# Softplus as one function of ScalarE in a selective-scan and int8 feed-forward layer

## What is computed

```python
u = layernorm(x)
xp = u @ x_proj_w.T                    # 96 columns: 64 for the step, 16 for B, 16 for C
delta = softplus(xp[:, :64] @ dt_proj_w.T + dt_proj_b)      # [row, 512]
dA  = exp(delta[..., None] * -exp(A_log))                   # [row, 512, 16]
dBu = delta[..., None] * Bm[:, None, :] * u[..., None]
h = dA_t * h + dBu_t                   # over the rows of a sequence, 512 x 16 states
y = sum_n h * C_t  +  u * D
x = x + y
x = x + int8_matmul(quantize(layernorm(x)), weight_q) * scales + bias
```

## Time and profile before

| | us |
|---|---|
| three runs | 3096.60, 3097.05, 3104.22 |
| median | 3097.05 |
| the profiled execution, its own time | 3105.25 |
| its span, first to last instruction | 3103.4 |
| steady stretch, 30 chunks (100.59 to 2942.38) | 2841.79, or 94.73 a chunk |
| busy in that stretch, a chunk: VectorE, ScalarE, TensorE, GpSimd | 92.85, 92.15, 87.00, 86.23 |

### The profile page before, as it was taken

How to read it: one execution, slowest core, us unless ns; L and a number is a source line. 1 busy time by engine, 2 the same in 40 slices (tenths; PEclk the granted TensorE clock), 3 DMA queues, 4 the chain that set the end, 5 groups by cost and what they waited for, 6 DMA issues and landing times.

```text
span 3103.4 us, 57860 instructions
## 1 busy us (share of the span) xinstructions
PE 2800.9 (90%) x21569; PEld 2423.8 (78%) x21632; DVE 2978.6 (96%) x3234; ACT 2952.2 (95%) x4930; POOL 2766.5 (89%) x1488
## 2 busy tenths in 40 slices
PE   5899999999999999999999899998999998999986
PEld 4778878788877788777887777887778877878875
DVE  5999999999999999999999999999999999999996
ACT  7999999999999999999999999999999999999984
POOL 3899989899899988999889998999889998899987
PEclk8999999999999999999999999999999999999998
DMA  4221222221222212222212222122222122221111
GB/s 151 66 79 56 79 80 79 80 92 42 80 92 79 79 57 79 79 79 93 79 43 79 93 79 79 58 78 80 79 82 91 42 82 90 79 79 66 56 65 41
DMA packets 111225, 236.01 MB, mean 76 GB/s; under 512 B 56097, under 2 KB 56097, under 8 KB 94562
## 3 DMA queue, kind: packets, MB, share of 16 engines
q1 hardware_dynamic: 110946, 232.32, 21.4%
HBM read 195.92 MB, written 36.37 MB: 75 GB/s over the span
## 4 chain that ended last, share of the span: by engine, by line
PE 31%; DVE 30%; ACT 29%; issue 9%; POOL 1%; DVEq 0%; POOLq 0%; ACTq 0%
DVE A L635 23%; ACT A L400 12%; ACT DB L413 10%; PE PB L519 9%; PE Y L538 9%; PE PB L516 6%; PE PM L559 3%; DVE ST L650 2%; DVE X L640 2%; ACT Z L465 2%; ACT QT L491 1%; ACT Z L461 1%; PE PM L550 1%; ACT C L483 1%; DVE AM L676 1%
## 5 line engine op out<-in xcount | busy, mean ns | idle before, releaser
L359 POOL TENSOR_TENSOR A<-A,CB 128x2048 f32<-128x2048 f32 x512 | 2327.9, 4560 | 17.8 <-DVE A L635 5.6
L635 DVE TENSOR_TENSOR_SCAN A<-A,CAR,PB 128x512 f32<-128x512 f32 x1536 | 1871.9, 1262 | 36.0 <-PE PB L519 12.5
L400 ACT ACTIVATE A<-DEL,an 128x512 f32<-128x512 f32 x2048 | 1366.5, 711 | 4.6 <-PE Y L538 3.0
L519 PE MATMUL PB<-idf,DB 128*128 128x128 f32 x6656 | 1030.7, 280 | 183.7 <-DVE A L635 175.1
L538 PE MATMUL Y<-idf,A 128*128 128x128 f32 x8192 | 1129.0, 275 | 2.0 <-POOL A L359 2.0
L413 ACT ACTIVATE DB<-XN,BC 128x512 f32<-128x512 f32 x1664 | 1113.1, 710 | 4.8 <-PE PB L519 2.7
L519 PEld LDWEIGHTS PB<-idf,DB 128*128 128x128 f32 x6656 | 768.8, 143 | 425.4 <-DVE A L635 306.3
L538 PEld LDWEIGHTS Y<-idf,A 128*128 128x128 f32 x8192 | 954.8, 143 | 32.6 <-issue 16.4
L635 DVE TENSOR_TENSOR_SCAN A<-A,PB 128x512 f32<-128x512 f32 x512 | 596.9, 1204 | 34.2 <-PE PB L519 14.4
L516 PE MATMUL PB<-DG,XN 128*128 128x128 f32 x3072 | 421.9, 281 | 50.9 <-DVE A L635 48.0
L516 PEld LDWEIGHTS PB<-DG,XN 128*128 128x128 f32 x3072 | 372.2, 191 | 87.1 <-issue 51.2
(11 more groups left out here) (69 smaller groups left out, 1678.3 us busy)
## 6 DMA issues: line engine op xcount, KB each, us to landing
CB<-c_rows SPq DMA_DIRECT2D x128, 1024.0 KB, 4.8
X<-in_x SPq DMA_DIRECT2D x32, 1024.0 KB, 5.6
out<-X SPq DMA_DIRECT2D x32, 1024.0 KB, 4.3
DG<-b_diag SPq DMA_DIRECT2D x32, 768.0 KB, 6.9
b_diag<-DG SPq DMA_DIRECT2D x2, 768.0 KB, 9.3
b_diag<-BC SPq DMA_DIRECT2D x96, 2.0 KB, 5.1
C<-in_wq SPq DMA_DIRECT2D x1, 1024.0 KB, 11.5
DB<-in_wq SPq DMA_DIRECT2D x1, 1024.0 KB, 13.3
```

The lines of the kernel that those rows point to most:

```text
L359: gp.tensor_tensor(A[s % NA][:, :, :], A[s % NA][:, :, :], CB[:, s % (4 * NG), :].unsqueeze(1).broadcast_to([128, KB, L]), ALU.mult).then_ ...
L400: act.activation(A[s % NA][:, g, :], DEL[k % 2][:, g, :], ACT.Exp, scale=an[:, g, n:n + 1])\
L519: i = pe.transpose(PB[u % 2][:, j * 128:(j + 1) * 128], DB[(scaled(s) - 1) % ND][:, j, g * 128:(g + 1) * 128], idf[:, :])
L635: dve.tensor_tensor_scan(A[s % NA][:, g, :], A[s % NA][:, g, :], PB[(4 * s + g) % 2][:, :], init, ALU.mult, ALU.add).then_inc(s_scan, 1)
```

## The change

The three tasks of ScalarE and the one of VectorE become one task of ScalarE, which reads PSUM and writes DEL. The buffer Z and three semaphores go. The waits that the VectorE pass had (for DEL's readers of two chunks ago) go over to ScalarE, and `d_t` now waits for ScalarE's pass.

```diff
 PLACES = {
-        "delta": (-356, -304, -239, -144),
+        "delta": (-283, -268, -228, -192),
...
-        Z = sb("Z", [128, 2, L])
...
-            def z_out(p, g):
-                n = KB * p + g
-                act.wait_ge(s_dt, n + 1)
-                if n >= 2:
-                    act.wait_ge(s_del, n - 1)
-                act.activation(Z[:, g % 2, :], bank(p, g)[:, :], ACT.Abs).then_inc(s_z, 1)
-
-            def sp_exp(p, g):
-                act.wait_ge(s_z, KB * p + g + 1)
-                act.activation(Z[:, g % 2, :], Z[:, g % 2, :], ACT.Exp, scale=-1.0).then_inc(s_e, 1)
-
-            def sp_ln(p, g):
-                act.wait_ge(s_e, KB * p + g + 1)
-                act.activation(Z[:, g % 2, :], Z[:, g % 2, :], ACT.Ln, bias=1.0).then_inc(s_ln, 1)
+            def delta(p, g):
+                act.wait_ge(s_dt, KB * p + g + 1)
+                if g == 0 and p >= 2:
+                    act.wait_ge(s_exp, 4 * NS * (p - 1))
+                    act.wait_ge(s_dlt, T * (p - 1))
+                act.activation(DEL[p % 2][:, g, :], bank(p, g)[:, :], ACT.Softplus).then_inc(s_del, 1)
...
-            def delta(p, g):
-                n = KB * p + g
-                dve.wait_ge(s_ln, n + 1)
-                if g == 0 and p >= 2:
-                    dve.wait_ge(s_exp, 4 * NS * (p - 1))
-                    dve.wait_ge(s_dlt, T * (p - 1))
-                dve.scalar_tensor_tensor(DEL[p % 2][:, g, :], bank(p, g)[:, :], 0.0, Z[:, g % 2, :],
-                                         ALU.max, ALU.add).then_inc(s_del, 1)
```

More of the change, by code:

```diff
@@ L7 @@
 PLACES = {
[L8 to L22, removed]
-        "delta": (-356, -304, -239, -144),
-        "dl_t": (-143, -113, -98, -92),
@@ L25 @@
[L25 to L51, removed]
[8 rows of a table removed]
[L60 to L67, removed]
+        "act_b": (-98, -93, -90, -89, -82, -82, -72, -72, -61, -34, -19, 20, 25, 29, 33, 33, 39, 124, 194,
@@ new lines @@
+        196, 198, 202, 210, 227, 317, 320, 321, 329, 334, 400, 428, 431, 445, 446, 450, 462, 463, 485, 490,
+        648, 654, 662, 713, 713, 714, 722, 728, 733, 753, 818, 888, 892),
+        "addbias": (1640,),
+        "amax": (1433, 1460, 1474, 1482),
+        "ascale": (1457,),
+        "b_c": (-451,),
+        "bc_out": (-368,),
+        "carry": (-12, 81, 163, 206, 331, 345, 428, 498, 508, 551, 630, 671, 675, 813, 834, 971),
+        "centre": (1287, 1295, 1296, 1398),
+        "d_t": (-331, -260, -255, -188),
@@ new lines @@
+        "decay": (-133, -107, -100, -91, -82, -77, -74, -62, -25, -22, -16, -15, 41, 49, 99, 99, 102, 104,
+        150, 155, 176, 185, 193, 197, 235, 237, 277, 278, 305, 317, 335, 376, 419, 430, 430, 448, 451, 505,
+        509, 529, 568, 584, 592, 609, 609, 647, 651, 688, 689, 699, 699, 716, 783, 792, 795, 796, 798, 806,
+        814, 815, 817, 847, 855, 859),
+        "delta": (-283, -268, -228, -192),
+        "dl_t": (-172, -141, -97, -78),
+        "du": (-84, -47, -36, -28),
+        "final": (2053, 2155),
@@ new lines @@
+        "gather": (1088, 1131, 1165, 1181),
+        "load": (-2162,),
+        "load_c": (-700, -667, -636, -486),
+        "load_g": (-670,),
+        "magic": (1529, 1555, 1584, 1590),
+        "newton0": (-1172,),
+        "newton1": (1175,),
+        "q_mm": (1785, 1826, 1884, 1930),
+        "q_t": (1569, 1605, 1631, 1700),
+        "qt_out": (1630, 1666, 1705, 1752),
+        "root0": (-1174,),
+        "root1": (1246,),
+        "scale_out": (1861, 1887, 1963, 2026),
+        "scales": (1586,),
@@ new lines @@
+        "scan": (29, 39, 41, 47, 54, 56, 56, 56, 66, 66, 74, 94, 119, 145, 154, 234, 244, 247, 255, 266, 283,
+        290, 291, 301, 307, 355, 368, 416, 432, 451, 462, 464, 538, 569, 591, 597, 598, 610, 611, 611, 618,
+        626, 626, 632, 634, 640, 661, 669, 757, 810, 819, 839, 844, 859, 873, 875, 940, 954, 954, 967, 973,
+        974, 984, 1016),
+        "stats0": (-1293, -1273, -1270, -1187),
+        "stats1": (1150, 1201, 1201, 1236),
+        "store": (1380,),
+        "store_c": (-883,),
@@ L68 @@
+        "store_g": (-901,),
[8 rows of a table added]
+        "times_c": (62, 142, 175, 299, 331, 371, 456, 531, 592, 620, 664, 690, 758, 876, 889, 972),
+        "weights": (-185,),
+        "x_p": (-557, -538, -512, -503),
+        "x_t": (-816, -715, -654, -634),
+        "xn": (-940, -932, -921, -921),
+        "xp_out": (-422,),
+        "xt_out": (-779, -718, -676, -641),
 }
@@ L185, in build @@
         s_dt = sem("s_dt")
-        s_z = sem("s_z")
-        s_e = sem("s_e")
-        s_ln = sem("s_ln")
         s_del = sem("s_del")
@@ L492, in qt_out @@
                                bias=-MAGIC).then_inc(s_qe, 1)
-            run(root0=lambda p, i: root(p, 0), root1=lambda p, i: root(p, 1), xn=xn, xt_out=xt_out, z_out=z_out,
-                sp_exp=sp_exp, sp_ln=sp_ln, xp_out=lambda p, i: xp_out(p), bc_out=lambda p, i: bc_out(p),
+            run(root0=lambda p, i: root(p, 0), root1=lambda p, i: root(p, 1), xn=xn, xt_out=xt_out, delta=delta,
+                xp_out=lambda p, i: xp_out(p), bc_out=lambda p, i: bc_out(p),
                 centre=centre, magic=magic, qt_out=qt_out, decay=decay, act_b=act_b)
@@ L689, in scale_out @@
                                          ALU.mult, ALU.mult).then_inc(s_o, 1)
-            run(stats0=lambda p, i: stats(p, 0, i), stats1=lambda p, i: stats(p, 1, i), gather=gather, delta=delta,
-                du=du, amax=amax, scale_out=scale_out, scales=lambda p, i: scales(p), weights=lambda p, i: weights(p),
+            run(stats0=lambda p, i: stats(p, 0, i), stats1=lambda p, i: stats(p, 1, i), gather=gather, du=du, amax=amax, scale_out=scale_out, scales=lambda p, i: scales(p), weights=lambda p, i: weights(p),
                 scan=scan)
```

## The result

| | before | changed |
|---|---|---|
| median of 4 runs, us | 3097.02 | 3280.02 |
| lowest to highest | 3096.60 to 3104.22 | 3279.30 to 3286.04 |
| the profiled execution and its span | 3105.25, 3103.4 | 3279.93, 3278.1 |

The ratio is 1.0583, with a 95% interval of 1.0564 to 1.0602. The forecast was 3261 us, with a range of 3185 to 3390.

What follows compares the result with a forecast made beforehand. VectorE and ScalarE were both taken as nearly full, with ScalarE setting the pace afterwards. Chunks of 100.06 us added 159.9 us over 30, edges 4, giving 3269.2, less 8.2 to the median: 3261 us, range 3185 to 3390.

Steps and rivals of the forecast that it cites:

- The bound: Steady chunks: VectorE and ScalarE both nearly full before; after, ScalarE sets the pace, VectorE's 2.4 us saving being worth nothing.
- What ScalarE loses and gains: ScalarE, per chunk: 4.76 us saved on Exp and Ln passes, 11.04 us added by eight table loads of 1.38.
- My sum without waits: Steady chunk: old period 94.73 us, less 4.76 for passes, plus 11.04 for loads, less 2.45 of old idle time.
- The waits: ScalarE's idle time per chunk: of 2.45 us, 1.5 kept, with ends 0.5 and 5.0; loads fill the wait before L423.
- The edges and the median: Outside the 30 chunks 4 us added for head and tail; 8.2 us taken off from profiled execution to median.
- The double stop: Rival at every ScalarE table switch: a second stop as long as the load, 321 us more, 3582 us; chance 0.07.
- New waits at the second and third softplus: Rival: tighter orders make ScalarE wait for the projection, idle 5.0 us a chunk in place of 1.5, 3366 us; chance 0.14.
- The limit: New orders: ScalarE may be at most 8, 4, 3 and 6 scans ahead at a chunk's four softplus passes.
- Hidden loads: Rivals on ScalarE: loads run beside other work, 3027 us, chance 0.04; or are partly hidden, 3110 to 3186 us, chance 0.06.

Runs made afterwards that it cites:

- e2_set: Changed kernel with the set holding Exp and Ln asked for again after each chunk's third and fourth softplus, four loads a chunk instead of eight: 3072.8 us, ratio 0.9895.
- e1_abs: Changed kernel with Abs in place of Softplus in the one pass, so no table loads in the chunks and no softplus computed: 3041.0 us, ratio 0.9790.
- e3_old_orders: Kernel before with its own orders, only the four softplus groups replaced by one Softplus pass each, twelve loads a chunk: 3404.5 us, ratio 1.0961.
- e11_fill_pause: Changed kernel plus 20 useless TensorE transposes a chunk ahead of the `tb` that waits at the first root: 3257.1 us, ratio 1.0507.
- e5_loads: Kernel before with all its passes, plus eight loads a chunk of the set that is loaded anyway: 3377.8 us, ratio 1.0875.

## Why the prediction was right

**The bound, right.** ScalarE sets the pace with 98.2 of 100.66 us, VectorE has 9.5 us to spare and waits for PB (174.2 us over 30 chunks, from TensorE) and A (77.5). Its work fell by 1.71 us a chunk and not by the 2.4 that I had reckoned, which changes nothing here.

**What ScalarE loses and gains, right within 0.3 us.** My sum without waits, 94.73 - 4.76 + 11.04 - 2.45, is 98.56; busy time and the gaps at the loads make 98.3. The Softplus pass takes 597 ns, as the Abs (588). A load cost 1.38 in the sum and 1.35 to 1.37 in three differences of busy time (changed to e2_set 5.46 for four, e1_abs to changed 10.84 for eight, changed to e3_old_orders 5.39 for four).

**The waits, mis-sized.** I kept 1.5 us of waits a chunk. Of the 2.48 us that ScalarE is idle 0.13 are the gaps at the loads, counted above, which leaves 2.35: 0.85 too few, or 26 us over 30 chunks. The step that failed is the reasoning behind it: I saw that the loads would fill the wait before L423 (it did go, from 41.8 us to 0.7 over 30 chunks), but priced a load only by the time it takes of ScalarE. Loads also delay what others wait for. The waits that grew are for A (27.9 us over 30 chunks, 2.2 before), XT (16.0, 6.0 before) and XP (14.9, none before), all from TensorE. e2_set traces those for A and XP to the roots' loads, and e11_fill_pause those for A to the pause at the first root and the fall of the clock behind it. Where the wait for XT comes from stays open: e2_set, without the roots' loads, still has 14.9 us of it.

**The edges and the median.** Head and tail came out at 258.3 us in place of the 265.6 that I had reckoned, 7 us less. And I took off 8.2 us because the profiled execution of the kernel before lay that far above its median; here it lay on the median, so that step alone accounts for 8 of the 19 us by which the forecast fell short. One profiled run on the high side says nothing about the next. The four misses are +26 for the waits, -8 for ScalarE's work, -7 for the edges and +8 for this step; that the sum is no further off than 19 us is in part luck, as two of them run against the others.

**The rivals.** The double stop is refuted by the gaps of 0.02 us, by e5_loads and by e2_set. The Trainium skill's "ScalarE: Activation LUTs", section "What ACT_TABLE_LOAD costs", gives 1283 ns for a load, which all 252 rows agree with, and 1380 ns of drain at every switch, which no row here shows; "ScalarE activation tables: per-element evaluation and per-set limits", section "What a function is on this engine", which has two sets one load apart, is what the runs bear out. New waits at the second and third softplus didn't come: 1.8 us in all at L454. The limit is real, though: without loads, in e1_abs, the wait for this projection is 49.9 us, at the second (35.7) and the fourth softplus (13.7) of the chunk. There ScalarE comes to them 4.0 and 5.1 decays ahead of the scans on average, in the changed kernel 3.6 and 3.8: under the loads VectorE catches up in part. Hidden loads are refuted by the rows.

## What to carry to other kernels

Before taking a function that replaces several passes, look in the built program for the loads of the function table and count them for each trip of the loop, also at functions that the change doesn't touch: here four of eight fell on roots whose functions the edit didn't touch, and one more line that asks for the common set (e2_set) turns the change from 5.8% slower into 1% faster. A load costs 1.36 us of the engine, and more if another engine stands waiting for what is queued behind it. Two functions of the loaded set in two passes (3049 us) beat one function from another set in one (3073 at best), for inputs at which exp(z) doesn't overflow.

## What the hardware showed that I had not expected

Chunks of equal work differed by 4%, in step with TensorE's granted clock. In the changed kernel the three steady chunks with a clock of 1.00 last 98.4 us on average, the three at 0.95 102.5. The chunk that starts at 1311.79 and the one that starts at 1413.12 have the same pause, 2.60 us:

```profile
1335.42 0.66 PE L504 MATMUL PB<-idf,DB 128*128 128x128 f32 x4 [2.60 <-ACT DB L406]
...
1436.75 0.66 PE L504 MATMUL PB<-idf,DB 128*128 128x128 f32 x4 [2.60 <-ACT DB L406]
```

In fine stretches, the first has behind it a mean clock of 0.67 over four us, and again 0.69 eight us later; the second keeps its clock. In the same columns as above:

```profile
1333.00:1337.00 4.00, 1.58 (x10) 1.23 (x11) 1.37 (x2) 4.00 (x7) 3.88 (x4) 0.91 0.00 0
1337.00:1341.00 4.00, 3.34 (x16) 2.31 (x15) 2.10 (x3) 4.00 (x8) 4.00 (x2) 0.67 0.00 0
1341.00:1345.00 4.00, 2.72 (x22) 2.08 (x21) 4.00 (x5) 4.00 (x7) 3.74 (x3) 1.00 0.00 0
1345.00:1349.00 4.00, 3.48 (x21) 3.25 (x20) 3.12 (x4) 2.58 (x5) 3.46 (x3) 0.69 0.12 43
1435.00:1439.00 4.00, 2.25 (x17) 1.81 (x18) 1.30 (x2) 4.00 (x7) 4.00 (x1) 1.00 0.02 6
```

In the first of the two chunks ScalarE waits for a buffer A until 1347.21, behind the first fall, in order of time (start us, duration us):

```profile
1347.21 1.33 ACT L393 ACTIVATE A<-DEL,an 128x512 f32<-128x512 f32 x2 [1.42 <-PE Y L523]
```

At either end of such a fall the clock goes between its two levels, 2.4 and 1.2 GHz. Why it falls behind one pause and not behind the same pause a chunk later stays open: the rows don't tell it, and no run here tests it. What was shown is that added useless transposes gave 18 us back where they stand exactly in the pause, and that more of them elsewhere cost 51.
